# Image steps of a conv, attention and expert kernel: the turned image copied before the normalisations, the weight cast moved to the middle of ScalarE's step, VectorE's weight subtraction behind the inverse roots

## What is computed

```
x = relu(x + softplus(s) * bn(conv1x1(relu(bn(conv3x3(relu(bn(conv1x1(x)))))))))
t = tokens(x)                                  # 16 x 196 tokens of 256
q, k, v = ln(t) @ w_qkv                        # 16 heads of 16
q = softmax(q / 4, axis=-1);  k = softmax(k, axis=tokens)
t = t + (v @ (q.T @ k per head)) @ w_out + b_out
n = ln(t);  p = softmax(n @ gate_w + gate_b)   # 8 experts, the best two
t = t + sum_e comb[e] * (gelu(n @ w1[e] + b1[e]) @ w2[e] + b2[e])
```

## Time and profile before

| | us |
|---|---|
| median of 3 runs | 734.79 (732.18 to 735.88) |
| the profiled execution | 728.51 |
| its span | 726.8 |
| TensorE busy | 610.5 (84%) |
| VectorE busy | 461.4 (63%) |
| ScalarE busy | 317.6 (44%) |
| GpSimd busy | 212.0 (29%) |

### The profile page before, as it was taken

How to read it: one execution, slowest core, us unless ns; L and a number is a source line. 1 busy time by engine, 2 the same in 40 slices (tenths; PEclk the granted TensorE clock), 3 DMA queues, 4 the chain that set the end, 5 groups by cost and what they waited for, 6 DMA issues and landing times.

```text
span 726.8 us, 14377 instructions
## 1 busy us (share of the span) xinstructions
PE 610.5 (84%) x3882; PEld 539.8 (74%) x3883; DVE 461.4 (63%) x1492; ACT 317.6 (44%) x626; POOL 212.0 (29%) x193
## 2 busy tenths in 40 slices
PE   6662589989889976149999999999999999999982
PEld 3641477777768965137998998998898899899872
DVE  2788799989898885515555555565564565555550
ACT  1645577867676542013433433333343334334330
POOL 5320121212755665711222122122122121221221
PEclk9876699999999995569999999999999999999996
DMA  9490888878877962421256372734626528322211
GB/s 278 131 345 2 323 313 298 302 258 296 292 282 259 372 236 75 135 55 30 40 161 189 84 251 45 269 77 127 208 44 177 169 38 293 54 37 44 30 16 15
DMA packets 50488, 120.83 MB, mean 166 GB/s; under 512 B 7564, under 2 KB 39184, under 8 KB 44304
## 3 DMA queue, kind: packets, MB, share of 16 engines
q1 hardware_dynamic: 30128, 98.07, 37.2%
q0 software_dynamic: 11136, 14.00, 11.5%
q10 hardware_dynamic: 9184, 8.28, 4.2%
HBM read 68.22 MB, written 52.11 MB: 166 GB/s over the span
## 4 chain that ended last, share of the span: by engine, by line
PE 58%; DVE 22%; issue 6%; ACT 5%; POOL 2%; DMA 2%; DVEq 2%; SPq 2%; ACTq 0%; POOLq 0%
PE ps L846 42%; PE ps L873 6%; DVE wset L1115 4%; PE ps L684 2%; DVE stt L1026 2%; POOL rows_by_expert L440 2%; PE ps L839 2%; PE ps L778 1%; PE ps L741 1%; ACT xh L540 1%; DVE tc L1017 1%; DMA wset<-in_ew 1%; DVE img L1109 1%; DVE bst L996 1%; PE ps L730 1%
## 5 line engine op out<-in xcount | busy, mean ns | idle before, releaser
L462 POOL DMA_INDIRECT out<-ys,xr x56 | 86.7, 1548 | 318.7 <-DVE ys L1382 248.4
L846 PE MATMUL ps<-wset,hTh 128*128 x896 | 163.6, 283 | 6.9 <-DVE hTl L1350 6.9
L846 PEld LDWEIGHTS ps<-wset,hTh 128*128 128x128 f32 x896 | 141.8, 190 | 14.9 <-issue 10.8
L846 PE MATMUL ps<-wset,xrTh 128*128 x448 | 147.4, 410 | 0.0
L635 ACT ACTIVATE hb<-hb 128x512 f32<-128x512 f32 x112 | 70.5, 632 | 140.1 <-DVE hb L1371 140.1
L846 PE MATMUL ps<-wset,hTl 128*128 x448 | 126.3, 282 | 0.0
L641 ACT CAST hTh<-ps 128x512 fp32r<-128x512 f32 x112 | 60.2, 590 | 102.4 <-PE ps L873 102.0
L1377 DVE TENSOR_TENSOR yb<-ps,bset 128x256 f32<-128x256 f32 x56 | 23.8, 424 | 124.6 <-PE ps L846 124.6
L846 PEld LDWEIGHTS ps<-wset,xrTh 128*128 128x128 f32 x448 | 81.1, 191 | 15.6
L846 PE MATMUL ps<-wset,xrTl 128*128 x224 | 89.5, 400 | 0.0
L1371 DVE TENSOR_TENSOR hb<-ps,bset 128x512 f32<-128x512 f32 x112 | 75.9, 685 | 16.8 <-PE ps L846 16.6
(11 more groups left out here) (181 smaller groups left out, 943.2 us busy)
## 6 DMA issues: line engine op xcount, KB each, us to landing
split_weights<-wset SPq DMA_DIRECT2D x16, 2048.0 KB, 7.4
wset<-split_weights SPq DMA_DIRECT2D x32, 1024.0 KB, 7.1
wset<-in_ew SPq DMA_DIRECT2D x16, 1024.0 KB, 10.1
xr<-rows_by_expert ACTq DMA_DIRECT2D x56, 132.5 KB, 2.2
bset<-in_eb SPq DMA_DIRECT2D x8, 640.0 KB, 9.1
img<-in_x SPq DMA_DIRECT2D x8, 392.0 KB, 6.4
out<-img SPq DMA_DIRECT2D x16, 196.0 KB
rows_by_expert<-rows,slot POOLq DMA_INDIRECT x64, 3.1
```

The source lines that it names most:

```text
L462: pool.indirect_dma_start(out, bass.IndirectOffsetOnAxis(xr[:, r % XR, C + E:ROW].bitcast(U32), 0), ys[:, r % YS, :], None, compute_op=ALU ...
L846: last = pe.matmul(dst, rows_k[:, k * 128:(k + 1) * 128], wset[:, bass.ds(column(k) + rest, width)], start=(k == 0 and n == 0), stop=(k == ...
```

## The change

Three lists are reordered; no instruction is added or removed. On ScalarE `in_keep` goes directly behind `in_relu`, and `split_leading` from behind the normalisations to between `soft_kT` and them. On TensorE `in_turn` goes from behind q to ahead of `soft_kT`. On VectorE `split_rest` goes from ahead of what is left of the inverse roots (and of `route_slots`, whose instructions are interleaved with it) to behind them.

```diff
@@ ScalarE
             for n in range(SLOTS_A):
-                for stage, do in (("soft", soft_v), ("soft", soft_exps), ("in", in_relu),
-                                  ("soft", soft_kT), ("norm2", lambda i: norm2_norm(i, n)),
-                                  ("norm", lambda i: norm_norm(i, n)), ("in", in_keep), ("ctx", ctx_proj)):
+                for stage, do in (("soft", soft_v), ("soft", soft_exps), ("in", in_relu), ("in", in_keep),
+                                  ("soft", soft_kT)):
+                    if 0 <= n - LAG[stage] < B:
+                        do(n - LAG[stage])
+                if n + EARLY < UNITS:
+                    split_leading(n + EARLY)
+                for stage, do in (("norm2", lambda i: norm2_norm(i, n)), ("norm", lambda i: norm_norm(i, n)),
+                                  ("ctx", ctx_proj)):
                     if 0 <= n - LAG[stage] < B:
                         do(n - LAG[stage])
                 if n >= ROUTE_LAG and n % 2 == 0 and (n - ROUTE_LAG) // 2 < B // 2:
                     route_exp((n - ROUTE_LAG) // 2)
-                if n + EARLY < UNITS:
-                    split_leading(n + EARLY)
@@ TensorE
-                for stage, lag, do in (("norm2", 1, norm2_logits), ("soft", 0, soft_kT), ("ctx", 0, ctx_ctx), ("qkv", 0, qkv_q),
-                                       ("in", 0, in_turn), ("ctx", 0, ctx_proj), ("qkv", 0, lambda i: qkv_kv(i, psK, C, "kexp1")),
+                for stage, lag, do in (("norm2", 1, norm2_logits), ("in", 0, in_turn), ("soft", 0, soft_kT), ("ctx", 0, ctx_ctx),
+                                       ("qkv", 0, qkv_q), ("ctx", 0, ctx_proj), ("qkv", 0, lambda i: qkv_kv(i, psK, C, "kexp1")),
@@ VectorE
                 if on["in"]:
                     in_mix(i["in"])
-                if EARLY <= n - 1 + EARLY < UNITS:
-                    split_rest(n - 1 + EARLY)
                 if n % 2 == 0 and g >= 1:
                     chains[1] = route_slots(g - 1)
                 for _ in chains[0]:
                     next(chains[1], None)
+                if EARLY <= n - 1 + EARLY < UNITS:
+                    split_rest(n - 1 + EARLY)
```

## The result

The changed kernel took 748.3 us (median of 4 runs, 746.87 to 748.76), the kernel before 734.27 beside it: a ratio of 1.0189, 95% interval [1.0157, 1.0221]. The profiled execution took 748.06 us with a span of 746.3. The forecast was -2.4 us, the measurement +14.0.

A forecast was written before the change was run, and what follows sets the result against it. The prediction took a ring of VectorE and ScalarE, from 70 to 236 us, to bound the kernel. A gain of 3.4 us, less 1.0 for TensorE's clock, gave -2.4 on 734.79: 732.4 us, range 727.0 to 738.5.

The forecast's parts named there:

- The start: Steps 1 to 4: cast(2) at about 87.3, VectorE's `kx` of step 4 at 99.05 for 97.55, a loss of 1.5 us.
- the clock: TensorE idles in step 2, so step 3's products may run at the low clock: between 0 and 2.5 us, taken as 1.0.
- The statistics' wait: VectorE's wait for ScalarE's copy before the statistics disappears: gain of 8.9 us over steps 7 to 15.
- The third rival: Nothing moves: TensorE takes up the wait, VectorE waits for `out_add` or `kx` instead; 0 gain, 734.8 us, chance 0.10.
- The late load: ScalarE's moved cast waits for its load, late by about 1 us; 2 to 3 us idle in step 12.
- the sum's +10.45: The cast's data come 10.45 us after the previous step's rest ends: 0.08 + 0.36 + 10.0.
- The 9.2 us: Skill page's time for 3 MB of store and load, where the rows say 10.4; by it no late cast after the start.
- its own ring: Rest, load, cast, normalisations, TensorE's `out_out`, `out_add` at 17.1, next rest: 21.9 us for two steps, 23.8 with slow landings.
- Then VectorE runs free: step 10 -0.85, step 11 -1.8, ...: After step 9 routed steps are set by VectorE's work, 22.7 us a pair; statistics of step 15 come 5.0 us early.
- Rival 2: Slower: every load lands like the last two, 12.0 us, deciding from about 11.0; +4.2 us, 739.0 us, chance 0.20.
- Rival 1: Full gain: loads land in time and the start loses nothing, no idle before the cast; -7.3 us, 727.5 us, chance 0.25.
- My sign of "wrong": Listed signs against the forecast included a granted TensorE clock of 0.50 beyond 102 us.

The follow-up runs named there:

- the runs with the early store: Changed kernel with its 2 MB store cut in two, the leading part stored once cast: 741.44 us, 1.0064; other kernels also carry this edit.
- mid_odd_late_even: Changed kernel with the leading part stored early and the cast ahead of the normalisations in odd steps alone, last in even steps: 726.46 us, 0.994.
- mid_even_late_odd: Changed kernel with the leading part stored early and the cast ahead of the normalisations in even steps alone, last in odd steps: 738.14 us, 1.0104.
- after: The changed kernel itself, with all three lists reordered, against the kernel before: 748.3 us, ratio 1.0189.
- late_hi: Changed kernel with ScalarE's cast put back behind ctx_proj and the routing's exponential, and the leading part stored early: 732.63 us, 0.9945.
- cast_back: Changed kernel with ScalarE's cast put back last, behind the normalisations; turn and copy early, rest behind the roots: 726.49 us, 0.9961.

## Why the prediction was wrong

**The start** was close up to `kx` of step 4. Load issued at 77.93 (77.0 predicted; the loop starts 0.85 later after, statistics at 71.35 for 70.50), cast(2) at 87.98 (87.3), `kx` of step 4 at 100.98. Less the 0.85 that is 100.1, where I had 99.05 and the old value was 97.55. The 1.0 too much is what I had allowed for the clock.

**The statistics' wait** went, as said: 9.9 to 1.4 us. But "Gain: 8.9 us" did not hold as a gain: turn and copy alone are 0.9988, with the rest behind the roots 0.9961, 1 to 3 us. The third rival ("nothing moves") was nearer to this part than the forecast, with another resource than it named: TensorE, which now waits for the relu in front of kT, `ctx_ctx` and q.

**The late load** was the right mechanism, "late by about 1 us", in the wrong steps. I put it in steps 7, 8 and 12; it came in steps 5 (1.48) and 8 (2.16). cast(5) starts 10.45 us behind the end of rest(4) (119.17 for 108.72), which is the sum's +10.45. Step 8's load took 12.02 us ahead of any scatter, a length that I had given only to loads beside scatters. The 9.2 us that the prediction also worked out for the 3 MB was met nowhere: in the ten profiles with the store of 2 MB, from 70 us on, the quickest load landed 9.43 us after its own issue, 9.8 after the store's. Its price was mis-sized: 9 us by the runs with the early store, from 3.6 us of waits after 95 us in the one profile. I priced it by its own ring and let VectorE win it back in routed steps. The waiting cast holds up the normalisations, and with them TensorE.

**The step that failed** is "Then VectorE runs free: step 10 -0.85, step 11 -1.8, ...", that is, routed pairs set by VectorE's 22.7 us of work. They are set by a ring that crosses three engines, TensorE's step after the odd turn, ScalarE's even step up to the exponential, VectorE's `route_top` to the relu. Three such pairs take 72.0 to 75.1 us without the cast on the ring and 78.5 to 80.8 with it, at the clock that goes with it; the forecast had 22.7 to 23.8 a pair. So the statistics of step 15 were 12.7 us late (237.58 for 224.93), not 5.0 early. The prediction's own list of what is queued behind the cast (normalisations, `ctx_proj`, xT copies) left out the exponential, though its text named a wait of 0.2 us for it in the earlier trace rows's step 11. mid_odd_late_even against mid_even_late_odd, 0.994 to 1.0104, shows that it is the even steps' cast; after the start one cast waits for a load in the latter (0.65 us in step 8) and none in the former. That the ring closes through the exponential is read from the chain.

**The sum.** I had -2.4; measured +14.0. (The recorded ring adds up to 17.0 us up to `out_add`, not 17.1; nothing hangs on it.) In ratios: order without the moved cast -0.4% (-2.9 us); moved cast with its load in time 0.9945 to 1.0064, +1.2% (some 8.7 us); late load +1.25% (9.2 us). Together -2.9 + 8.7 + 9.2 = +15.0 us, measured 14.0. The missing -1.2 us is the early store with the cast late (0.9961 to 0.9945). With it the four terms are steps of one path from the kernel before to "after" and add up of necessity, so the sum confirms none of them; each is uncertain by some 0.3 to 0.4%.

**The rivals.** Rival 2 (739.0) had the right sign and place, and stopped at the load. It decides from a landing of 11 us "in all steps"; two late loads were enough. Rival 1's sign did not come: two casts did idle for their loads. My sign of "wrong", a clock of 0.50 beyond 102 us, was there at 167 and 194 us (0.54 at 128 to 130), and rival 3's, VectorE's idle time under another name, in part. The range ended at 738.5, since every case let routed steps recover.

**What stays open.** All casts in the middle (1.0064) should cost at least as much as the even ones alone (1.0104); the intervals overlap, and nothing here decides whether that is chance. Nor is the clock's share known better than 0 to 5 us. No version came out clearly below 0.994: mid_odd_late_even (0.994) and late_hi (0.9945) are the best and equal, both with the early store.

## What to carry to other kernels

Before an instruction is moved ahead in an engine's list, list everything that it now stands in front of, and for each the engine that waits for the result, even where that wait is 0.2 us in the old profile: here that small wait marked an item that was on the ring. Price a ring through all its engines over its whole period (here two steps), not one engine's busy time. And an instruction that waits for a transfer belongs behind those that the ring waits for: here the cast behind the exponential cost nothing that could be told, and ahead of it 0.7 to 2.3%.

## What the runs showed of the hardware that was not expected

- A load of 1 MB behind a store of 2 MB landed after 12.02 us with no indirect transfer in flight (for the cast of step 8), where the median of its kind from 100 to 160 us was 10.0; before, only loads beside scatters took 11.8 to 12.0. The lateness sat in one of its sixteen parts: by the trace's semaphore events fifteen had landed 10.0 us after the issue, and the last at 155.18. A packet of 16 KB of the queue that the page calls "instruction" (q8) began at 153.15. Of the 204 loads of a matrix from 70 us on whose landings are whole, in all 19 profiles, 23 had a last part 0.8 us or more behind the fifteenth; in 22 of these a 16 KB packet of q8 began in the 5 us before that part landed, and in 24 of the other 181. That is a meeting in time and no more: nothing was changed to test it.
- The length of a wait of TensorE did not tell by itself whether the granted clock fell. Around all six turns shown here that had waited 3.03 to 3.19 us it was 0.50 to 0.60 for some 4 us. Behind waits of 1.91 to 1.95 us it stayed at 1.00 in mid_odd_late_even, and fell for 2 to 4 us in "after" at 128 us (0.54) and in cast_back at 158 us (0.50). Sixteen identity products inside the wait kept it at 1.00, and returned less (3.0 and 2.1 us over three such turns, and nothing that the runs tell) than the doubled durations of kT, `ctx_ctx` and q suggest (1.06 for 0.60, 1.91 for 1.06, 2.98 for 1.89).
